# Batch 0's expert logits with the gate matrix stationary and early, and batch 1's row sends in waited pairs, in a selective-scan plus mixture-of-experts kernel

## The reference

```
h = _layernorm(x, axis=-1) * (1 + ca) + sa
x = x + ga * _L0_attn_ref(h, ...)          # the scan; per state k: h = dA*h + dBu, y += h*C
h = _layernorm(x, axis=-1) * (1 + cb) + sb
# the experts:
gate_logits = einsum('bsd,de->bse', h, gate_kernel)           # 256 x 8
top_k_weights, top_k_indices = top_k(gate_logits, 2)
top_k_weights = softmax(top_k_weights)
inter = silu(h @ w0[e]) * (h @ w1[e])                         # 256 -> 512
out = sum over the two experts e of weight_e * (inter @ wo[e])  # 512 -> 256
x = x + gb * out
```

## Time and profile before

| | |
|---|---|
| median of 3 runs | 844.09 us (843.63 to 844.12) |
| the profiled execution's own time | 846.63 us |
| its span in the profile | 844.8 us |
| mean granted TensorE clock | 0.957 of full speed |
| PE busy | 729.5 us, 86% |
| DVE busy | 622.4 us, 74% |
| POOL busy | 512.9 us, 61% |
| ACT busy | 338.3 us, 40% |

### The profile page before, as it was taken

One profiled execution on the slowest core, in us unless ns is written; L12 is line 12 of the kernel. 1 busy time (PEld: TensorE's weight loads), 2 busy tenths in 40 slices (PEclk: granted clock), 3 DMA queues, 4 the chain that ended last, 5 costly groups with the idle time before them and its releaser, 6 DMA issues. The chain is left out here.

```text
span 844.8 us, 9320 instructions
## 1 busy us (share of the span) xinstructions
PE 729.5 (86%) x2249; PEld 366.9 (43%) x2250; DVE 622.4 (74%) x824; ACT 338.3 (40%) x382; POOL 512.9 (61%) x271
## 2 busy tenths in 40 slices
PE   5799998878797897978989889895698999999994
PEld 2444343323232332323435334374364666666663
DVE  4478888999999998999999998865253544444442
ACT  0777866445553543535536464212111111111110
POOL 1012233999999999999999998946622222222222
PEclk9899999999999999999999998996999999999998
DMA  9364643876767666676969979685542222222220
GB/s 285 86 169 148 188 158 112 226 182 163 206 157 189 181 170 182 182 187 173 247 179 272 244 167 254 178 260 170 179 106 52 43 45 35 48 47 38 46 30 1
DMA packets 62298, 126.43 MB, mean 150 GB/s; under 512 B 11898, under 2 KB 33850, under 8 KB 62140
## 3 DMA queue, kind: packets, MB, share of 16 engines
q1 hardware_dynamic: 50468, 116.12, 50.6%
q0 software_dynamic: 7152, 8.48, 5.9%
q10 hardware_dynamic: 4648, 1.48, 0.7%
HBM read 98.08 MB, written 24.69 MB: 145 GB/s over the span
## 5 line engine op out<-in xcount | busy, mean ns | idle before, releaser
L1690 POOL TENSOR_TENSOR pool<-pool,hT 128x1024 f32<-128x1024 f32 x92 | 214.7, 2356 | 12.8 <-PE PS L699 12.8
L1079 ACT ACTIVATE PS<-pool,negA 128x1024 f32<-128x1024 f32 x128 | 143.1, 1118 | 181.3 <-DVE pool L1388 181.3
L699 PE MATMUL PS<-pool,ident 128*128 128x512 f32 x368 | 185.2, 628 | 25.9 <-POOL pool L1690 25.1
L1773 POOL DMA_INDIRECT out<-uT,ptab x39 | 60.6, 1555 | 169.2 <-DVE uT L1616 160.2
L1388 DVE TENSOR_TENSOR_SCAN pool<-PS,pool 128x1024 f32<-128x1024 f32 x64 | 143.1, 2273 | 0.4 <-ACT PS L1079 0.4
L900 PE MATMUL PS<-pool,uT 128*128 (+1 forms) x312 | 142.7, 601 | 0.0
L699 PEld LDWEIGHTS PS<-pool,ident 128*128 128x128 f32 x368 | 67.8, 195 | 104.1 <-issue 52.6
L681 PE MATMUL PS<-pool 96*128 96x512 bf16 x256 | 78.5, 388 | 33.2 <-DVE pool L1376 17.6
L1590 DVE TENSOR_TENSOR uT<-uT,PS 128x512 f32<-128x512 f32 x39 | 26.9, 689 | 88.2 <-PE PS L900 80.3
L1690 POOL TENSOR_TENSOR Y<-pool,hT 128x1024 f32<-128x1024 f32 x36 | 84.0, 2357 | 2.2 <-DVE pool L1388 1.3
L1714 POOL TENSOR_TENSOR spread<-spread,pool 128x1024 f32<-128x1024 f32 x32 | 75.4, 2355 | 14.7 <-ACT spread L1085 14.4
(11 more groups left out here) (199 smaller groups left out, 862.6 us busy)
## 6 DMA issues: line engine op xcount, KB each, us to landing
hT<-C_scratch SPq DMA_DIRECT2D x128, 512.0 KB, 5.3
pool<-in_w SPq DMA_DIRECT2D x16, 512.0 KB
uT<-expert_in_scratch SPq DMA_DIRECT2D x39, 130.5 KB
Y<-Y SPq DMA_DIRECT2D x32, 128.0 KB, 2.4
C_scratch<-Y SPq DMA_DIRECT2D x8, 512.0 KB, 2.6
pool<-du_scratch SPq DMA_DIRECT2D x8, 512.0 KB, 6.6
Y<-in_wo SPq DMA_DIRECT2D x8, 512.0 KB
expert_in_scratch<-zrow SPq DMA_DIRECT2D x16, 130.5 KB, 6.4
```

The costliest lines, as they stand in the source:

```text
L699: m = pe.matmul(PS[:, 6 + half, :], ident[:, :], prod_k[:, HF * half:HF * half + HF], start=False, stop=k == DS - 1)
L1079: act.activation(pair(2 * (k % 2)).unsqueeze(1), delta[:, chunk_at(g2, r), :], ACT.Exp, scale=decay[:, bass.ds(g2 * (2 * DS) + n, 1)]).the ...
L1690: gp.tensor_tensor(to, hst[:, k % HR, :], crep[k % RC], ALU.mult).then_inc(prod_done, 1)
L1773: gp.indirect_dma_start(out=out, out_offset=bass.IndirectOffsetOnAxis(ap=ptab[:, slot:slot + 1], axis=0), in_=yo[:, slot % 2, :], in_offse ...
```

## The change

- **Logits of batch 0.** `first_logits` now has the gate stationary (128x8) and streams `h2T`: 4 matmuls of 512 columns, as third piece of the last chunk, right after the transposes. They give the logits turned (8 x 1024, banks 6 and 7). ACT copies them to `lgT` (after its decays of step 5, waiting for the matmuls), and the chunk's own sums, which use the same banks, now wait for that copy. `CATCH_UP` has an entry for three pieces. At the second-last step PE turns `lgT` back by 8 small transposes (`turned_logits`), then does `turned_back`, which stood behind the ranks; `ranks(0)` now stands ahead of the very last sum.
- **Behind the scan.** ACT moves batch 0's rows before the exponentials and the last copy of the scan; DVE does weights and places before `gate_y`.
- **POOL.** Batch 0's sends are split 10, 5, 1 about the two `rstd_of`, not 5, 5, 6. Batch 1's sends go in pairs, and each pair but the first waits until all sends ahead have landed.
- **Ranks of batch 1** stand on PE behind the first two row turns and the hidden layer of slot 0; ACT's `gap_exp(1)` stands behind those slots' moves.
- **Tails.** ACT writes the zero rows four at a time, after the hidden layers of slots 3 and 4.
- **yo** has four buffers, of which two serve slots 0 and 1 alone. `yo_free` starts at 4, and POOL raises it from slot 3 on.

```diff
@@ -193,6 +193,7 @@
...
         xn2 = [uT[:, 3, :].rearrange("p (t n) -> p t n", t=TQ), uT[:, 2, :].rearrange("p (t n) -> p t n", t=TQ)]
+        lgT = uT[0:NE, 2, :]
         h2T = uT[:, 0:2, :].rearrange("p c n -> p (c n)").rearrange("p (t k n) -> p t k n", t=NTB, k=KD)
@@ -230,7 +231,7 @@
...
         intT = take(2 * MLP).rearrange("p (r k n) -> p r k n", r=2, k=KM)
-        yo = take(2 * DM).rearrange("p (r n) -> p r n", r=2)
+        yo = take(4 * DM).rearrange("p (r n) -> p r n", r=4)
         gsel = take(2 * DM).rearrange("p (r n) -> p r n", r=2)
@@ -666,7 +667,7 @@
...
-            CATCH_UP = {0: (), 2: (4, 6), TQ: (6, 8, 10, 11)}
+            CATCH_UP = {0: (), 3: (6, 8, 10), TQ: (6, 8, 10, 11)}
@@ -750,14 +751,20 @@
...
             def first_logits():
+                pe.wait_ge(t1_done, NTB)
+                for half in range(2):
+                    for k in range(KD):
+                        m = pe.matmul(PS[0:NE, 6 + half, :], gate_sb[:, k, :], h2T[:, TQ * half:TQ * half + TQ, k, :],
+                                      start=k == 0, stop=k == KD - 1)
+                    m.then_inc(g_mm, TQ)
+
+            def turned_logits():
+                pe.wait_ge(lg0_done, 1)
                 pe.wait_ge(dbu_done, 1 + NG * OWN)
                 pe.wait_ge(spread_in, NG * len(SHARED))
-                pe.wait_ge(t1_done, NTB)
                 for t in range(NTB):
-                    for k in range(KD):
-                        m = pe.matmul(PS[:, 4, NE * t:NE * t + NE], h2T[:, t, k, :], gate_sb[:, k, :],
-                                      start=k == 0, stop=k == KD - 1)
-                    m.then_inc(g_mm, 1)
+                    m = pe.transpose(PS[:, 4, NE * t:NE * t + NE], lgT[:, P * t:P * t + P], ident[0:NE, 0:NE])
+                m.then_inc(lg0_done, 1)
@@ -806,7 +814,11 @@
...
                     if last and k == DS - 2:
-                        first_logits()
+                        turned_logits()
+                        for j in range(NTB // 2):
+                            turned_back(j)
+                    if last and k == DS - 1:
+                        ranks(0)
                     for _ in range(sums_at[k]):
@@ -832,10 +844,7 @@
...
-            blocks_behind(NB + 1, 1, [lambda i=i: turned_pair(i) for i in range(2)], True)
-            ranks(0)
-            for j in range(NTB // 2):
-                turned_back(j)
+            blocks_behind(NB + 1, 1, [lambda: turned_pair(0), lambda: turned_pair(1), first_logits], True)
@@ -873,10 +882,7 @@
...
                     outward_1(t, k)
-            for q in range(1, NQ):
-                scored(q)
-                ranks(q)
-
+            scored(1)
@@ -926,6 +932,7 @@
...
             hidden(0, 0, 0)
+            ranks(1)
             for s2 in range(NE // 2):
@@ -1158,6 +1165,9 @@
...
                     take_turned(2 * (k - LAG + 1) + 1)
+                if g == CH + 3 and k == LAG + 1:
+                    act.wait_ge(g_mm, NTB)
+                    act.activation(lgT, pair(6)[0:NE], ACT.Copy).then_inc(lg0_done, 1)
@@ -1179,14 +1189,12 @@
...
+            for j in range(NTB // 2):
+                take_rows2(j)
             gap_exp(0)
             leave(NG // 2 - 1, 1)
-            for j in range(NTB // 2):
-                take_rows2(j)
-            for q in range(1, NQ):
-                for t in range(*GROUPS[q]):
-                    take_h2(t)
-                gap_exp(q)
+            for t in range(NTB, NT):
+                take_h2(t)
@@ -1203,6 +1211,7 @@
...
             take_rows(0, 1)
+            gap_exp(1)
             silu_h(0, 0)
@@ -1212,11 +1221,11 @@
...
                     silu_h(s2 + r, 1 - r)
-                    if s2 in (1, 2):
-                        if s2 == 1 and r == 0:
+                    if s2 == 1:
+                        if r == 0:
                             act.wait_ge(known, 2)
-                        tail(4 * (s2 - 1) + 2 * r)
-                        tail(4 * (s2 - 1) + 2 * r + 1)
+                        for i in range(NE // 2):
+                            tail(NE // 2 * r + i)
             with act.Fori(NE // 2, SPAIRS) as s2:
@@ -1455,7 +1464,10 @@
...
                 tiles, n = slice(first, end), end - first
-                dve.wait_ge(g_mm, end)
+                if q:
+                    dve.wait_ge(g_mm, end)
+                else:
+                    dve.wait_ge(lg0_done, 2)
                 if q == 0:
@@ -1536,9 +1548,9 @@
...
             pick(0)
-            gate_y(NG - 1)
             weights(0)
             place_of(0)
+            gate_y(NG - 1)
             step(dve.tensor_copy(ef[:, 0:NE], iota8[:, :]))
@@ -1613,7 +1625,7 @@
...
                 dve.wait_ge(yo_free, s2 * 2 + (r + 1))
-                dve.scalar_tensor_tensor(yo[:, r, :], PS[:, 6 + r, 0:DM], wtab[:, slot], gsel[:, r, :],
+                dve.scalar_tensor_tensor(yo[:, r if not (isinstance(s2, int) and s2 == 0) else 2 + r, :], PS[:, 6 + r, 0:DM], wtab[:, slot], gsel[:, r, :],
                                          ALU.mult, ALU.mult).then_inc(yo_done, 1)
@@ -1653,7 +1665,7 @@
...
             gp.wait_ge(nhalf_done, 1)
-            gp.sem_inc(yo_free, 2)
+            gp.sem_inc(yo_free, 4)
@@ -1748,20 +1760,21 @@
...
             gp.wait_ge(placed, 1)
-            send(0, slice(0, 5))
+            send(0, slice(0, 10))
             rstd_of(2)
-            send(0, slice(5, 10))
+            send(0, slice(10, 15))
             rstd_of(3)
-            send(0, slice(10, 16))
+            send(0, slice(15, 16))
             gp.wait_ge(ysum_done, RC + NG * DS)
...
             gp.wait_ge(noted, 4)
-            for q in range(1, NQ):
-                gp.wait_ge(placed, q + 1)
-                send(q, slice(0, 2 * NTB))
-
-            for q in range(1, NQ):
-                gp.wait_ge(sent[q], 16 * 2 * NTB)
+            gp.wait_ge(placed, 2)
+            for i in range(2 * NTB):
+                if i % 2 == 0 and i:
+                    gp.wait_ge(sent[1], 16 * i)
+                send(1, slice(i, i + 1))
+
+            gp.wait_ge(sent[1], 16 * 2 * NTB)
             gp.sem_inc(arrived, 1)
@@ -1769,9 +1782,10 @@
...
                     gp.wait_ge(added, 16 * slot)
+                if slot > 2:
                     gp.sem_inc(yo_free, 1)
                 gp.indirect_dma_start(out=out, out_offset=bass.IndirectOffsetOnAxis(ap=ptab[:, slot:slot + 1], axis=0),
-                                      in_=yo[:, slot % 2, :], in_offset=None, bounds_check=T - 1, oob_is_err=False,
+                                      in_=yo[:, slot % 2 + 2 * (slot < 2), :], in_offset=None, bounds_check=T - 1, oob_is_err=False,
                                       compute_op=ALU.add).then_inc(added, 16)
```

More of the change, by code:

```diff
@@ L272, in adaln_mamba_moe @@
         col_in = sem("col_in")
-        nmr_done, xn2_done, t1_mm, t1_done, t2_mm, t2_done, tables = (
-            sem(n) for n in ("nmr_done", "xn2_done", "t1_mm", "t1_done", "t2_mm", "t2_done", "tables"))
+        nmr_done, xn2_done, t1_mm, t1_done, t2_mm, t2_done, tables, lg0_done = (
+            sem(n) for n in ("nmr_done", "xn2_done", "t1_mm", "t1_done", "t2_mm", "t2_done", "tables", "lg0_done"))
         ident_by_in, wdt_in, wz_in, placed_w = (sem(n) for n in ("ident_by_in", "wdt_in", "wz_in", "placed_w"))
```

## The result

The changed kernel is **slower: ratio 1.0088 (95% interval 1.0070 to 1.0106)**, 853.9 us median of 19 runs (848.7 to 859.5) against 846.9 of 19 runs of the kernel before (843.6 to 851.8) on the same chip. That is +7.4 us by the ratio (7.0 between the two medians). The forecast was +3.6 us, 847.7 in a range of 842.5 to 854.5: the sign and the range held, the size was half of what came. The three runs known before the prediction lay near the low end of what that kernel does, so 853.9 stands close to the top of the range; the ratio on the 844.09 from which the range was worked out gives 851.5.

What follows compares the result with a forecast made beforehand. Prediction: PE's output of slot 6 decides, held by POOL's paired sends and the scatters behind them; the steps put it at 652.6 instead of 648.97, +3.6 on the 844.09 median, giving 847.7 us, range 842.5 to 854.5.

Steps and rivals of the forecast that it cites:

- Step 1: Logits inside the scan's last chunk: ACT's copy and late spreads of B delay the scan by 1.4 us (0 to 3).
- Step 2: End of the scan: sends of batch 0 start at 554.9, 3.6 us earlier than 558.50.
- Steps 3 and 4: More sends ahead of each rstd (22.85 us to its end) and ranks behind slot 0: batch 1's sends 6 us later, 593.5.
- Step 5: Batch 1's pairs of sends: landing 3.0, restart 0.8, 5.07 us a pair; first scatter at 633.7 against 609.97.
- 4.4 to 6: Sign on batch 1's pairs: the prediction is wrong if they come under 4.4 us apart or over 6.
- Step 6: yo buffers: slot 4's result waits for three scatter landings, 9.95 us, until 643.6; output of slot 6 at 652.6, +3.6.
- POOL is not what decides: Rival for the slots: both known gaps are really removed, slot 6's output 11 us earlier, 833; chance 0.12.
- Sends land quickly: Rival on the pairs: landings of 2.6 us throughout, first scatter at 631.0, +0.9, 845.0; chance 0.22.
- Loaded landings: Rival on the pairs: the first two or three take 6.4 us, first scatter 7 to 10 later, 854.5 to 858; chance 0.13.
- 6.87 us wait: PE's wait before slot 1's output: no separate case, since it would fall inside the time PE stands for POOL.
- free pipeline: The faster case where POOL does not decide: slot 6's output at 638, -11, 833 us; left out of the range.

Runs made afterwards that it cites:

- best1: Changed kernel with scatters of slots 0 to 3 between the pairs, batch 0's sends 5, 5, 6 and batch 1's ranks ahead of slot 0; ratio 0.9826.
- pairs_alone: Kernel before with nothing changed but sends going in pairs, each pair waiting for those ahead; ratio 1.0115.
- yo6: Changed kernel with six yo buffers in place of four, so slots 0 to 5 need no scatter; ratio 1.0092.
- scan_alone: Kernel before with only the early logits and the reordered end of the scan; sends, ranks, zero rows and yo as before; ratio 0.9957.
- twelve: Changed kernel, but batch 1's sends go twelve, one wait, then four; ratio 0.9913 to the kernel before.
- eights: Changed kernel, but batch 1's sends go eight at a time, with one wait behind the eighth; ratio 0.9951 to the kernel before.
- best2: best1 with batch 1's sends four at a time and scatters of slots 0, 1 and 2 behind the 8th, 12th and 16th send; ratio 0.9820.
- best2_tails2: best2 with the zero rows written two at a time, behind slots 3 to 6, as before; ratio 0.9879.
- best3: best1, but batch 1's sends go twelve, one wait, four, and only slot 0's scatter stands among them, behind the twelfth; ratio 0.9810.

## Why the prediction was right, and where its size was off

- **Step 1** (+1.4): measured +0.6 on average, but in three levels, -1.3, +0.3 and +1.6; the changed kernel's profile has +0.3. ACT's copy was nearly hidden there, the range's lower end. What chooses the level was not tried.
- **Step 2** (first send 3.6 us earlier, net of step 1): the piece from the last products is 5.3 shorter, where the working had 5.0. Net -4.7 on average, where the forecast had -3.6.
- **Steps 3 and 4**: `rstd_of(3)` ends 22.4 us behind the first send, not 22.85; batch 1's sends start 37.5 behind it, not 38.6 (38.2 to 39.8 in the six other runs with this order). Right, and best1 shows that this order is a loss of its own: 5 to 8 us together with what it does to slot 2's rows.
- **Step 5** (40.2 us from the first send to the first scatter): 41.4 here, 44.3 and 36.9 in the other two runs where the scatters stand behind the pairs. The middle of the pairs was right (5.22 us apart on average, not 5.07), but partly by luck: two terms were off and cancel. By the semaphore events in the trace the second send of the first seven pairs landed after 3.7 us on average, not 3.0, and POOL's next send then began after 0.27, not 0.8; only the first scatter took 0.95. Nor is a pair a constant: it took 3.95 us when nothing went beside it and 6.7 beside the first weight loads, both outside the 4.4 to 6 that the prediction named as the bounds of being right. In the changed kernel ACT's four zero rows at a time fall beside the fifth and sixth pairs (5.4 each; in pairs_alone, with two at a time, the three pairs beside them took 4.0, 4.1 and 4.7). My range for this step took in the loads, not the change's own zero rows. The Trainium skill (DMA: Bandwidth & Descriptors, section Anatomy of one DMA — SWDGE (gpsimd) path) fits a DMA that GpSimd issues as 2.0 us plus its bytes over 436 GB/s, which for such a send is an estimate of 2.3 us. The trace comes near it only with nothing beside the send: the quiet landings of waited sends in these runs are 2.4 to 2.8, and beside the first 512 KB loads they are 4.9 to 5.4.
- **Step 6 is where the size failed.** I took 3.55 us between scatters, from the last two of the kernel before; they follow after 4.6. That is 3 x 1.05 = 3.2 us too little, and result of slot 4 came 13.2 us behind the first scatter, not 9.9. From there to slot 6's output it was 9.0, as said. The row was badly chosen: the last scatters of that kernel carry no rows. The DMA view of the kernel before, 825 to 845 us,

```profile
DMA packets 434, 0.03 MB, mean 1 GB/s; under 512 B 432, under 2 KB 432, under 8 KB 432
out<-uT,ptab POOLq DMA_INDIRECT x3, 2.7
```

  has three scatters, 0.03 MB in all, that land in 2.7 us; the same view of the changed kernel, 628 to 650 us, has

```profile
DMA packets 912, 0.93 MB, mean 42 GB/s; under 512 B 112, under 2 KB 880, under 8 KB 912
out<-uT,ptab POOLq DMA_INDIRECT x5, 3.8
```

  3.8 us was also in the earlier trace rows, for the median of all 39, and 3.8 + 0.8 of restart, as in step 5, would have given 4.6.
- **The sum.** By measured terms: -4.7 for the scan, and a path of 101.0 instead of 90.3, +10.7: **+6.0**, and up to 3 us more where the pairs run as in yo6. The runs say +7.4 (5.9 to 9.0 by the interval). The same sum (-4.7 where a run has the new logits, plus its path less 90.3) comes within 3 us of the ratio of each of the other runs but yo6, whose wait lies behind slot 6. The forecast's path was 97.7; of the 3.3 us that it lacks, step 6 is 3.3, while steps 3 and 4 (1.1 too long) and step 5 (1.2 too short) cancel. In the profiled execution a scan that ended early hid part of it (+4.6), so its absolute times met the forecast within a us (643.52 for 643.6, 652.52 for 652.6) by two errors that cancel.
- **The rivals.** "POOL is not what decides" falls: 19.33 us of DVE's idle time. "Sends land quickly" holds for the quiet pairs alone (2.4 to 2.6) and falls for the sum. "Loaded landings" is partly true, 1 to 4 us of it, not 7 to 10. I wrote that the 6.87 us wait was no separate case. For this kernel's time that is right, since it would fall under POOL's wait. For what the pairs are worth it is not: without them the kernel stands at 0.9968, not at the 833 us of the free pipeline, because the wait comes back.

## What to carry over

When an engine's fixed program gets waits put in, ask what stands behind the last one, not only what each costs: with the same waits the kernel with this change is 0.9% slower than the one before when the scatters stand behind them, and 0.7% faster when the scatters stand between them. Take the price of a repeated transfer from a row that moves the same bytes; a kernel's last rows may move none. Read a gain in a stretch against a mark inside the same execution: the start of the scan's last chunk differed by up to 5 us from one profile to another, more than most of the terms here.

## What was not expected of the hardware

With sixteen sends of 134 KB issued by GpSimd in a row, PE's signals to DVE and ACT arrived late in all three profiles with such a row (outputs of slots 0 and 1 12.9, 10.9 and 11.3 us apart), from 13 to 15 us behind the first send until 4 to 5 behind the last. The latest seen, ACT's for slot 2 in the kernel before, is 8.5 us behind the end of the work (603.05 to 611.53). The semaphore events in the traces show that the signals were held and not the work. In scan_alone PE's signals for work that its records end at 601.84, 602.28, 604.00 and 605.71 are at 609.48, 609.54, 609.60 and 609.66. Work done late would have left 1.7 us between the last two, as these records have. DVE's own signals meanwhile are in time (one for work that ended at 601.07 is at 601.08).

With a wait behind every second, fourth or eighth send, or one behind the twelfth, the outputs of slots 0 and 1 came 5.82 us apart in six profiles of six in the change's order, in pairs_alone and in best1. Not every signal was prompt even there: in twelve the one for DVE's copy of slot 1 was 1.7 us late, which the slots' own slack took in, and in eights the result of slot 2 came 1.2 us late. In best1's order with groups of four or twelve (best2, best2_tails2, best3) signals were late again, with smaller gaps: two outputs came 10.3, 7.3 and 8.8 us apart, one place in each. (The 7.6 us behind that gap in best2 and best3 is PE at a granted clock of 0.50 to 0.54.) So the number of sends under way is not the whole of it. Which of sends, weight loads and zero rows has to meet was not tried, and the cause stays open.
